# Computing the last layer's state space parameters on GpSimd during the last batch of the first block, in place of VectorE at its end

## The reference

```python
Lam = Lam_re + 1j * Lam_im                      # 64 states
dt = jnp.exp(log_step)
Lam_bar = jnp.exp(Lam * dt)
B_bar = ((Lam_bar - 1.0) / Lam)[:, None] * (B_re + 1j * B_im)
Bu = jnp.einsum('bld,pd->blp', u, B_bar)
xs = scan of  x[l] = Lam_bar * x[l-1] + Bu[l]
y  = 2.0 * jnp.einsum('blp,dp->bld', xs, C_re + 1j * C_im).real + D_diag * u
```

## Time and profile before

| | |
|---|---|
| time, median of 3 runs | 2064.86 us (2064.7 to 2066.64) |
| the profiled execution's own time | 2067.85 us |
| its span | 2066.0 us |
| PE busy | 1786.0 us (86%), 8463 matmuls |
| DVE busy | 1365.8 us (66%), 2947 instructions |
| ACT busy | 1109.4 us (54%), 2117 instructions |
| POOL busy | 582.1 us (28%), 775 instructions |

### The profile page before, as it was taken

How to read it: one execution, slowest core, us unless ns; L and a number is a source line. 1 busy time by engine, 2 the same in 40 slices (tenths; PEclk the granted TensorE clock), 3 DMA queues, 4 the chain that set the end, 5 groups by cost and what they waited for, 6 DMA issues and landing times. The chain is left out here.

```text
span 2066.0 us, 25670 instructions
## 1 busy us (share of the span) xinstructions
PE 1786.0 (86%) x8463; PEld 1057.7 (51%) x8463; DVE 1365.8 (66%) x2947; ACT 1109.4 (54%) x2117; POOL 582.1 (28%) x775
## 2 busy tenths in 40 slices
PE   2376577999999999658989999999999998599998
PEld 1155355766767666413344545454444445367666
DVE  5746888988887553467877686868686721675650
ACT  6634667877876553114575657575656573122221
POOL 0235746755654421020000101010101101244442
PEclk9756788999999999857999999999999999699999
DMA  9440000000000020033030303030303003100000
GB/s 374 117 138 2 26 1 19 19 1 19 14 4 11 11 73 1 16 61 61 5 64 4 64 4 64 5 64 5 64 5 64 4 6 102 41 11 21 11 21 21
DMA packets 94422, 83.57 MB, mean 40 GB/s; under 512 B 9881, under 2 KB 87842, under 8 KB 94034
## 3 DMA queue, kind: packets, MB, share of 16 engines
q1 hardware_dynamic: 94192, 81.91, 14.6%
q10 hardware_dynamic: 98, 0.03, 0.0%
HBM read 51.26 MB, written 5.09 MB: 27 GB/s over the span
## 5 line engine op out<-in xcount | busy, mean ns | idle before, releaser
L2117 DVE TENSOR_REDUCE l_small<-l_psum 128x1 f32<-128x512 f32 x512 | 329.8, 684 | 137.9 <-PE l_psum L2079 132.9
L1905 ACT ACTIVATE l_prob<-l_psum 128x512 f32<-128x512 f32 x512 | 286.4, 596 | 229.5 <-PE l_psum L1956 226.2
L1894 POOL TENSOR_TENSOR k_x_res<-k_x_res,k_arena_a 128x256 f32<-128x256 f32 x32 | 23.2, 726 | 469.1 <-DVE k_arena_a L2161 469.1
L1965 PE MATMUL l_psum<-l_prob,l_v 128*32 128x512 f32 x1024 | 138.1, 612 | 0.2
L2026 PE MATMUL l_psum<-k_arena_a,l_gu 128*128 128x256 f32 x512 | 134.1, 390 | 0.7 <-ACT l_gu L1921 0.7
L2079 PE MATMUL l_psum<-k_arena_b 96*128 96x512 bf16 x256 | 105.1, 444 | 22.8 <-DMA k_arena_b<-k_arena_c 12.0
L88 PE MATMUL l_psum<-l_turned_over,k_arena_a 128*128 128x512 f32 x256 | 120.4, 596 | 4.2 <-ACT l_gu L1921 4.2
L1338 PE MATMUL l_psum<-l_w_f,k_arena_b 128*128 128x256 f32 x512 | 118.6, 380 | 1.0 <-ACT k_arena_b L1152 1.0
L88 PE MATMUL l_psum<-k_arena_b,l_w_f 128*128 128x512 f32 x256 | 119.5, 600 | 0.0
L88 PE MATMUL l_psum<-l_hT,k_arena_b 128*128 128x512 f32 x256 | 117.3, 605 | 0.9 <-ACT l_hT L2314 0.9
L2368 PE MATMUL l_psum<-k_arena_b,l_gu 128*128 128x256 f32 x512 | 113.2, 379 | 0.0
(11 more groups left out here) (380 smaller groups left out, 3835.4 us busy)
## 6 DMA issues: line engine op xcount, KB each, us to landing
su_raw<-in_L_cond_wa SPq DMA_DIRECT2D x6, 1536.0 KB, 21.9
k_arena_b<-k_arena_c SPq DMA_DIRECT2D x32, 192.0 KB, 3.5
k_x_res<-in_x SPq DMA_DIRECT2D x1, 4096.0 KB, 19.4
k_arena_b<-k_arena_c SPq DMA_DIRECT2D x32, 128.0 KB, 3.2
out<-k_x_res SPq DMA_DIRECT2D x8, 512.0 KB
l_mod_mlp<-mod SPq DMA_DIRECT2D x8, 384.0 KB, 3.6
l_qT<-k_arena_c SPq DMA_DIRECT2D x16, 192.0 KB, 3.5
l_kT<-k_arena_c SPq DMA_DIRECT2D x16, 192.0 KB, 3.2
```

Of the source, the lines that this page charges most:

```text
L1894: pool.tensor_tensor(x_tile(e, n), x_tile(e, n), add2[:], ALU.add).then_inc(x_ready.sem, 1)
L1905: act.activation(prob[:, s % 2, j, :], psum[:, 2 + n % 2, :], ACT.Exp, scale=float(HD) ** -0.5).then_inc(exp_ready.sem, 1)
L1965: last = pe.matmul(psum[j * BLOCK:(j + 1) * BLOCK, 4, :], v[e % 2][:, kt, at:at + BLOCK], prob[:, n % 2, j, :], start=(kt == 0), stop=(kt ...
L2117: dve.tensor_reduce(mx[:, n % T, n // T:n // T + 1], psum[:, n % 2, :], AX.X, ALU.max).then_inc(max_ready.sem, 1)
```

## The change

All of the `s5p` work of DVE but the two copies out of PSUM goes to POOL. GpSimd is not given the fused scalar_tensor_tensor, so each of those becomes two instructions, and the reciprocal becomes a power of minus one.

- POOL: piece 0 (24 instructions, up to the angles) stands after `rmsh` of batch 7, at pipeline step 5. Pieces 1 to 4 (80 instructions: the nine doublings with 6 each, B_bar, the output matrix, the D columns) stand right after `rgg` of batch 7 at step 6, before `root4` of batch 7 in that step.
- ACT: the two sines stand after `gelu` 7 of batch 5, before `hT` 0 of batch 6.
- PE: the three transposes stand after `turn2` 0 of batch 7, before `f2` 0 of batch 6, and use PSUM bank 2.
- DVE: only the two copies are left, after `x3` 1 of batch 6.
- SP: the 13 loads are issued at `load_style` of batch 7, when the layer 0 transposes of batch 7 are done; the stores stay where they were in the queue.
- The buffers are in `junk_h`, `junk[3]` and an unused end of arena_a, in place of arena_c.

```diff
 POOL_TURN = (
-    ("rgg", 0, 1), ("sgn", 1, 3), ("s5p", 1, -3), ("hw", 0, 2), ... ("mx", 0, 5), ("s5p", 0, -2),
-    ("xo", 0, 3), ... ("rmsh", 0, 2), ("fac", 0, 3), ("root", 0, 6), ("x2", 0, 2),
+    ("rgg", 0, 1), ("s5p", 1, 1), ("s5p", 2, 1), ("s5p", 3, 1), ("s5p", 4, 1), ("sgn", 1, 3), ("hw", 0, 2), ... ("mx", 0, 5),
+    ("xo", 0, 3), ... ("rmsh", 0, 2), ("s5p", 0, 2), ("fac", 0, 3), ("root", 0, 6), ("x2", 0, 2),
     ("root4", 0, 1), ...
 ACT_TURN = (
-    ... ("gelu", 7, -3), ("proj", 0, 1),
+    ... ("gelu", 7, -3), ("s5p", 0, -1), ("proj", 0, 1),
     ("hT", 0, -2), ...
 PE_TURN = (
-    ("up", 7, 0), ("s5p", 0, -8), ("merge", 2, -1), ...
+    ("up", 7, 0), ("merge", 2, -1), ...
-    ("hq", 6, 0), ("turn2", 0, -1), ("hq", 7, 0), ("f2", 0, -2), ...
+    ("hq", 6, 0), ("turn2", 0, -1), ("s5p", 0, -1), ("hq", 7, 0), ("f2", 0, -2), ...
 ...
 # sync
                     elif stage == "load_style":
+                        if e == B - 1:
+                            sp.wait_ge(turned.sem, turned.at(e, T))
+                            sp.wait_ge(o_turned.sem, o_turned.at(e, T))
+                            ... the 13 loads, each .then_inc(s5_loaded, 16)
 ...
                 sp.wait_ge(add2_ready.sem, add2_ready.at(B - 1, T))
-                ... the 13 loads
 # gpsimd
+                        s5 = Chain(pool, s5_step)
                         if t == 0:
                             pool.wait_ge(s5_loaded, 16 * S5_LOADS)
 ...
+                            for k in range(DOUBLINGS // 2) if t == 1 else range(DOUBLINGS // 2, DOUBLINGS):
+                                w = 2 ** k
+                                s5.link(gp.tensor_scalar(tmp[:, 0:w], sinT[:, 0:w], sn[:, k:k + 1], None, ALU.mult))
+                                s5.link(gp.tensor_scalar(cosT[:, w:2 * w], cosT[:, 0:w], cs[:, k:k + 1], None, ALU.mult))
+                                s5.link(gp.tensor_tensor(cosT[:, w:2 * w], cosT[:, w:2 * w], tmp[:, 0:w], ALU.subtract))
+                                s5.link(gp.tensor_scalar(tmp[:, 0:w], cosT[:, 0:w], sn[:, k:k + 1], None, ALU.mult))
+                                s5.link(gp.tensor_scalar(sinT[:, w:2 * w], sinT[:, 0:w], cs[:, k:k + 1], None, ALU.mult))
+                                s5.link(gp.tensor_tensor(sinT[:, w:2 * w], sinT[:, w:2 * w], tmp[:, 0:w], ALU.add))
 ...
+                            s5.link(gp.tensor_tensor(sq[:, 5:6], sq[:, 4:5], inverse, ALU.pow))
 ...
+                            gp.tensor_scalar(w_out, c_same, sgnum, -2.0, ALU.mult, ALU.mult)
+                            gp.tensor_scalar(sinT, sinT, sgnum, None, ALU.mult)
+                            s5.link(gp.tensor_scalar(bb, b_swap, sq[:, 8:9], None, ALU.mult))
+                            s5.link(gp.tensor_scalar(b_same, b_same, sq[:, 0:1], None, ALU.mult))
+                            gp.tensor_tensor(bb, b_same, bb, ALU.add).then_inc(bb_ready, 1)
+                            ... three products for the D columns
+                            pool.wait_ge(bb_ready, 2)
 # vector
-                        ... all pieces but the last
+                        dve.wait_ge(bb_turned, 2)
+                        V.tensor_copy(w_in, psum[:, 2, 0:KD * P]).then_inc(s5_done, 1)
+                        V.tensor_copy(skip_rows, psum[0:2 * KD * B, 2, tok(KD)]).then_inc(s5_done, 1)
```

More of the change, by code:

```diff
@@ L609 @@
     ("amaxh", 0, -2), ("u", 3, -1), ("h", 5, -2), ("base", 1, -3), ("hw", 1, -2), ("merge", 1, -3), ("h", 6, -2), ("amaxh", 1, -2), ("h", 7, -2),
-    ("amaxh", 2, -2), ("base", 2, -3), ("hw", 3, -2), ("s5p", 1, -4), ("merge", 2, -3), ("mods", 0, -1), ("amaxh", 3, -2), ("qsh", 0, -2),
-    ("amaxo", 0, -1), ("base", 3, -3), ("qso", 0, -1), ("qhT", 0, -2), ("qhT", 1, -2), ("qs", 0, 0), ("s5p", 2, -4), ("qoT", 0, -1), ("qoT", 1, -1),
+    ("amaxh", 2, -2), ("base", 2, -3), ("hw", 3, -2), ("merge", 2, -3), ("mods", 0, -1), ("amaxh", 3, -2), ("qsh", 0, -2),
+    ("amaxo", 0, -1), ("base", 3, -3), ("qso", 0, -1), ("qhT", 0, -2), ("qhT", 1, -2), ("qs", 0, 0), ("qoT", 0, -1), ("qoT", 1, -1),
     ("add2", 0, -2), ("merge", 3, -3), ("setup", 0, 0), ("qhT", 2, -2), ("add1", 0, -1), ("qhT", 3, -2), ("qoT", 2, -1), ("add1", 1, -1),
     ("qoT", 3, -1), ("add2", 1, -2), ("add1", 2, -1), ("qhT", 4, -2), ("add1", 3, -1), ("qhT", 5, -2), ("qT", 0, 0), ("stats2", 0, -1),
[4 rows of a table removed]
[3 rows of a table added]
 H_AT, XW_AT = 0, T * FF
 ARENA_A = T * FF + T * 3 * D
+S5_AT = 3 * KD * D + KD * D + KD * FF + KF * D + 2 * T * D // 16
 GU_AT, XT_AT, HT_AT = 0, KF * L, KF * L + KD * L
@@ L835, in _ @@
                     elif stage == "load_style":
+                        if e == B - 1:
+                            sp.wait_ge(turned.sem, turned.at(e, T))
+                            sp.wait_ge(o_turned.sem, o_turned.at(e, T))
+                            pre = "L3_cond_"
+                            for at in (slice(0, NS), slice(NS, P)):
+                                for i, name in enumerate(("Lam_re", "Lam_im", "log_step")):
+                                    sp.dma_start(lam[at, i:i + 1], io[pre + name].rearrange("(p a) -> p a", a=1)).then_inc(s5_loaded, 16)
+                            for dst, lo, hi in ((b_same, "B_re", "B_im"), (b_swap, "B_im", "B_re"), (c_same, "C_re", "C_im")):
+                                sp.dma_start(dst[0:NS, :], io[pre + lo]).then_inc(s5_loaded, 16)
+                                sp.dma_start(dst[NS:P, :], io[pre + hi]).then_inc(s5_loaded, 16)
+                            sp.dma_start(d_col, io[pre + "D_diag_col"]).then_inc(s5_loaded, 16)
                         if e:
@@ L878, in _ @@
                 sp.wait_ge(s5_done, 2)
-                for at, n, src in ((W_IN_AT, 2 * D, MX_AT), (COS_AT, 2 * L, TH_AT), (DECAY_AT, 2, MX2_AT + D)):
-                    sp.dma_start(prep3[:, at:at + n], arena_c[:, src:src + n]).then_inc(s5_stored, 16)
+                for at, n, src in ((W_IN_AT, 2 * D, arena_a[:, S5_AT:S5_AT + 2 * D]), (COS_AT, 2 * L, junk_h[:]),
+                                   (DECAY_AT, 2, arena_a[:, S5_AT + 3 * D:S5_AT + 3 * D + 2])):
+                    sp.dma_start(prep3[:, at:at + n], src).then_inc(s5_stored, 16)
                 sp.dma_start(skip3, skip_rows).then_inc(s5_stored, 16)
@@ L987, in _ @@
-                            pool.wait_ge(consts_ready, 3)
-                            gp.tensor_tensor(ex[:, 0:1], euler[:, 0:1], lam[:, 2:3], ALU.pow).then_inc(dt_ready, 1)
-                        else:
-                            pool.wait_ge(angle_ready, 1)
-                            gp.tensor_tensor(decay, euler[:, 0:1], ex[:, 1:2], ALU.pow).then_inc(decay_ready, 1)
+                            s5.link(gp.memset(euler, 2.718281828459045))
+                            s5.link(gp.memset(inverse, -1.0))
@@ new lines, in _ @@
+                            s5.link(gp.memset(sgnum[0:NS, :], -1.0))
+                            s5.link(gp.memset(sgnum[NS:P, :], 1.0))
+                            s5.link(gp.tensor_tensor(ex[:, 0:1], euler[:, 0:1], lam[:, 2:3], ALU.pow))
+                            s5.link(gp.tensor_tensor(ex[:, 1:2], lam[:, 0:1], ex[:, 0:1], ALU.mult))
+                            s5.link(gp.tensor_tensor(decay, euler[:, 0:1], ex[:, 1:2], ALU.pow))
+                            s5.link(gp.tensor_tensor(ex[:, 2:3], lam[:, 1:2], ex[:, 0:1], ALU.mult))
@@ new lines, in _ @@
+                            for k in range(DOUBLINGS):
+                                last = gp.tensor_scalar(ang[:, k:k + 1], ex[:, 2:3], float(2 ** k), None, ALU.mult)
+                            s5.link(last)
+                            s5.link(gp.tensor_scalar(turns[:], ang[:], 1.0 / TWO_PI, ROUND, ALU.mult, ALU.add))
+                            s5.link(gp.tensor_scalar(turns[:], turns[:], ROUND, None, ALU.subtract))
+                            s5.link(gp.tensor_scalar(cs[:], turns[:], -TWO_PI_HI, None, ALU.mult))
@@ L1276, in _ @@
                         for k in range(KD):
-                            last = turn(nc, psum[:, 0, tok(k)], bb[:, tok(k)], ident[:])
+                            last = turn(nc, psum[:, 2, tok(k)], bb[:, tok(k)], ident[:])
                         last.then_inc(bb_turned, 1)
-                        turn(nc, psum[0:2 * KD * B, 1, 0:P], skip_cols.rearrange("p a b -> p (a b)"), ident[:]).then_inc(bb_turned, 1)
+                        turn(nc, psum[0:2 * KD * B, 2, tok(KD)], skip_cols.rearrange("p a b -> p (a b)"), ident[:]).then_inc(bb_turned, 1)
                     elif stage == "turn":
```

125 lines of the change are left out of this document (42 added, 83 removed), and 18 rows, old and new, of tables (ACT_TURN, DVE_TURN, PE_TURN, POOL_TURN).

## The result

The changed kernel takes 2085.04 us (median of 4 runs, 2081.4 to 2086.13) against 2064.78 us (2062.78 to 2066.64) for the kernel before: a ratio of 1.0095, 95% interval 1.0078 to 1.0113, or 16 to 23 us more. It is slower, as forecast, and by more than the range allowed: forecast was 2075.8, from 2069 to 2083.

A forecast was written before the change was run, and what follows sets the result against it. PE, busy 86% of the span, was taken as the bound. Delay at `f2` 13.4 us and clock loss 1.9, with the shorter tail, put the block end 10.9 later: 2064.86 becomes 2075.8 us, range 2069 to 2083.

The forecast's parts named there:

- the chain with 0.06 us to spare: From `root4` through `yn` to TensorE's `turn2` 0 of batch 7: claimed to have only 0.06 us of slack.
- The tail, 4.2 us: Block end: copies, transposes and stores leave the path, so it ends with the last `x3`; 4.2 us gained.
- Piece 0 and the sines: GpSimd before `x2`: 6 to 7 us in an 8.08 us hole; sines and table load 0.7 us on ACT; no cost.
- Pieces 1 to 4, 30.6 us: GpSimd after `rgg` of batch 7: 80 instructions, 29.1 us plus 1.5 of waiting for DVE, ending at 809.0, delaying `root4`.
- the turns with VectorE: GpSimd waits up to 0.4 us at each of DVE's four `base` steps of batch 7: 1.5 us in all.
- The hole, its clock and the sum behind it: PE idles before `turn2` 0: `root4` 12.6 us late, `f2` 13.4 late, low clock 1.9 more; block end 10.9 us later.
- From the profiled execution to the median: Whole program: profiled 2067.85 would become 2078.8; the median lies 3 us under it, so the forecast was 2075.8.
- A: Rival, chance 0.17: same mechanism, GpSimd's pointer scalars and wide tensor_scalar dearer, 36 to 39 us; time 2081 to 2084.
- B: Rival, chance 0.13: GpSimd's added work at its floor, 27 us, no waits for DVE, clock back in 3.7 us; 2071.
- C: Rival, chance 0.04: GpSimd's added work fits into the 18.0 us before `root4`, only the block end's saving counts; 2060.7.
- D: Rival, chance 0.07: clock doesn't fall in the shorter hole before layer 2, 2 to 3 us come back; 2073.
- E: Rival, chance 0.03: GpSimd's first piece overruns its 8.08 us or a load is late, ACT stands at the sines; 2078 and up.

The follow-up runs named there:

- e2_pe_early: Kernel before, with only TensorE's three `s5p` transposes moved from the end of its queue to between two `f2` of batch 7; 2067.68 us, ratio 0.9996.
- e3_forms: Kernel before, with 37 linked GpSimd instructions added behind its others in the block: a memset and six forms at three widths; one execution, 2071.92 us.
- e9: Kernel before, with the three `s5p` transposes moved into `f2` of batch 7 and 40 unread identity transposes on TensorE before layer 2; 2059.81 us, ratio 0.9963.

## Why the prediction was right or wrong

**What bounds the kernel, and the chain with 0.06 us to spare.** Right. `root4`, `yn`, `turn2` became the path, and every microsecond of delay was one on the end.

**The tail, 4.2 us.** Right between the marks (4.27 in e2_pe_early). "What follows is unchanged" held in the changed kernel (1214.64 for 1214.95), but not in general: in the other six executions with the short tail what follows took 0.8 to 3.0 us longer.

**Piece 0 and the sines.** Right in what they cost the end: GpSimd needed 735.72 to 742.35, 6.6 us, and `x2` still waits 1.51 us for VectorE. The table load and the sines took 1.5 us on ScalarE (751.02 to 752.52), twice the 0.7 of the forecast, but TensorE shows no wait from 748.28 until 767.39.

**Pieces 1 to 4, 30.6 us.** Wrong, and this is the step that made the forecast miss: the mechanism held, and this term of the sum was too small. Measured 37.85:

| | forecast | measured |
|---|---|---|
| doublings | 20.0 and 1.5 of turns | 26.5 (780.09 to 806.59) |
| head of piece 1 | 0.9 | 0.9 |
| piece 3 | 4.4 | 4.9 |
| piece 4 | 3.8 | 5.5 |

I had priced a wide tensor_scalar by the nearest row with one input, the cast of the earlier trace rows, at 0.84 ns a column, and had as the upper end the 2.1 ns of two inputs. It costs 2.5: the four doublings' forms over 511 columns and piece 4 hold 4 x 511 + 1024 columns of it, times 1.66 ns, 5.1 us. The two-operation w_out of piece 4 did cost what I took for all. The other part is the scalar from SBUF: the steps start 0.37 to 0.40 us apart and not 0.31, for some 46 instructions 2.8 to 4.1 us. I named this price, from 2 to 4.6 us, and left it out of the sum because no row showed it, which put it at nothing; that such a scalar has a price of its own was also among the signs that I gave for the prediction being wrong. Against these stand some 0.8 us that were too much: the turns with VectorE. Four small instructions, one at each `base` step, were longer than their like by 0.1 to 0.2 us, 0.7 in all against 1.5 forecast.

**The hole, its clock and the sum behind it.** The form was right. `root4` late by 12.6 us was to give 13.4 and 1.9; late by 19.8 it gave, by the marks, 22.1. The clock cost the first 16 `f2` 2.1 us, forecast 1.9. It came back some 6 us after TensorE took up work, inside the 3.7 to 7.6 of the two rows that I had (the first is rather 4.0: 0.76 in 781 to 782 puts the change near 781.5). Put 37.9 for 30.6 in the sum: 10.9 + 7.3 = 18.2 us. Between the marks, where the sum belongs, 17.8 were measured. That the whole executions differ by 18.3 (2086.13 for 2067.85) fits even better by luck: 0.8 of it lie ahead of `rgg`, and 0.3 less behind.

**From the profiled execution to the median.** I took 3 us off because the profiled execution of before lay 3 us over its median. That of the changed kernel lies 1.1 over its own. This is 1.9 of the 9.2 us by which the forecast missed; the other 7.3 are the term above. How far one profiled execution lies from a median of a few runs is chance that the step took for a constant.

**The rivals.** A was the one: "GpSimd dearer", 36 to 39 us and 2081 to 2084; measured 37.85 and 2085.04. "One tensor input should not cost two" was the argument against it, and the rows of e3_forms refute it; the 2.5 ns a column are even above the 2.1 that A took as the upper bound. B and C are out by the same rows. D is out too: the hole before layer 2 was 6.98 us and the clock fell in it all the same (0.53 in 871 to 872); the eight transposes behind it took 1.97 us as before. To have it back for them took work for TensorE in the hole (e9). E did not happen.

## What to carry to other kernels

When work is moved into an engine's idle time, look at what that engine's next instruction releases: 18 us of idle time were there, but they ended in a chain with 0.06 us to spare, and behind that chain stood TensorE. Price an instruction that the trace does not have by its own form, with its number of operations and where its scalar lies, or measure it first: 37 probe instructions in a place that nobody waits for cost nothing between the marks here. And microseconds saved just ahead of a hole of TensorE may not be kept behind it: here 4.3 us did not show in the time until TensorE was given work in the hole.
